# Mamba scan loop: the C rows by broadcast DMA from a DRAM scratch in place of a spread on TensorE and a copy on ScalarE

## Chip, cores and metric

The kernel runs on one core of a Trainium2 chip. The metric is device microseconds of one execution, the median of several. Engines: TensorE (PE in the rows; PEld is its weight load), VectorE (DVE), ScalarE (ACT), GpSimd (POOL), and the sync engine SP, which here only issues DMAs.

## What is computed

The reference is a network of four layers, each a mixer and an expert part. The change lies in the first mixer, a Mamba block on x of shape (2, 1024, 128) with 256 channels and 16 states:

```python
x_dbl = xs @ x_proj_w.T                       # 256 -> 64 + 16 + 16
dt, Bm, Cm = jnp.split(x_dbl, [DT_RANK, DT_RANK + D_STATE], axis=-1)
dt = jax.nn.softplus(dt @ dt_proj_w.T + dt_proj_b)
A = -jnp.exp(A_log)
def step(h, inp):
    dt_s, B_s, C_s, x_s = inp
    dA = jnp.exp(dt_s[..., None] * A)
    h = h * dA + (dt_s * x_s)[..., None] * B_s[:, None, :]
    y = jnp.einsum('bds,bs->bd', h, C_s)
    return (h, y)
...
y = jnp.transpose(ys, (1, 0, 2)) + D_param * xs
```

## The kernel before

Channels lie on the 128 partitions, the 2048 tokens (two sequences of 1024) along the row; four blocks of 512 tokens are called k = 0 to 3, a PSUM bank holds one block. Each engine has its own hand-written program; semaphores of the group m0 tie them together. `m0["dve"]`, `m0["act"]` and `m0["pe"]` are counters with named offsets.

Ahead of the scan, per block k: TensorE projects xs (L379) into two banks, 64 rows of dt and 32 rows of B and C. ACT copies dt to `dt_low` (L458). VectorE splits the 32 rows into three bf16 parts in `parts` (L548 to L552, the semaphore value `bc`), whose sum is the fp32 value. The banks are used in turn, so blocks 2 and 3 wait for block 0 and 1 to be read. Then ACT loads the table for exp and ln (L459). For each of eight (block, channel half) pairs TensorE projects dt (L389), ACT makes log(1 + exp(-|x|)) with three instructions (L467 to L469) and VectorE finishes delta with two (L561, L562). Four products `dtx` (L566) follow, delta times xs.

The scan loop has 64 units (b, m, n): sequence, channel half, state; each covers 128 channels and 1024 tokens. In one unit:

- TensorE spreads row n of B to all 128 partitions: two matmuls (one per half of the tokens) of a 0/1 selector with `parts` (L395), into the banks BMM; then likewise row n of C, into the banks CMM.
- ACT makes the decay exp(delta A) in two PSUM banks (L479), and copies the C banks to one of two buffers CB in `shared` (L484).
- VectorE makes the drive, dtx times B (L573), and the scan (L576), in one of four state buffers.
- GpSimd multiplies the states with C (L592).
- TensorE adds the product up in PSUM with an identity (L405, fp32), over the 16 states of a (b, m).

VectorE may reuse a state buffer when the sum of the unit four before is made; ACT copies a sum out every 16 units. After the loop come the skip term and the gate (L579, L580) and the output projection. SP loads later weights into `shared` after the gate.

## Time and profile before

| | us |
|---|---|
| median of 3 runs | 1453.62 |
| lowest, highest | 1451.54, 1453.8 |
| the profiled execution | 1451.61 |
| its span | 1449.9 |
| scan loop, first drive to last scan's end | 250.2 to 477.1 |

The span is the time from the first to the last instruction of the profiled execution. The times in rows are from its start; "idle before" is how long an engine stood still ahead of an instruction, and behind the arrow is what it waited for. TensorE's clock is given as a share of 2.4 GHz. fp32 matmuls appear as two instructions each.

### The profile page before, as it was taken

The page shows a single profiled execution, that of the slowest core. Times are in us where ns is not written, and L with a number is a line of the kernel's source. Part 1 is how long each engine was busy: PE and PEld are TensorE (multiplying, and loading weights), DVE is VectorE, ACT ScalarE, POOL GpSimd, SP SyncE. Part 2 cuts the span into 40 slices and gives each one's busy share as a digit, 9 for nine tenths or more (in the row PEclk, how much of TensorE's full clock was granted, in tenths as well). Part 3 has the DMA queues.
Part 4 walks back from the last instruction along what each step waited for, and adds up shares of the span by engine and source line. Part 5 has one row for each costly group of instructions (what it writes and reads, how often), then busy time and mean ns, then how long its engine had stood idle before and what let it go on. Part 6 is the DMA issues. An engine that isn't in the chain of part 4 may idle for free.

```text
span 1449.9 us, 14958 instructions
## 1 busy us (share of the span) xinstructions
PE 1249.0 (86%) x5185; PEld 623.9 (43%) x5185; DVE 1042.3 (72%) x1535; ACT 825.7 (57%) x1061; POOL 442.5 (31%) x231
## 2 busy tenths in 40 slices
PE   5889976888888659999995799999999999888887
PEld 1333321222222234544452566666656666522454
DVE  4555468999999846464346889999989999833354
ACT  4434455565565224342235778888888888644642
POOL 9000000666666830000000135454444545510000
PEclk8899997999999859999997899999999999999999
DMA  3000000000000300000000000000000000000000
GB/s 109 1 0 0 1 0 1 0 0 0 1 0 0 137 0 0 1 0 1 0 0 0 10 18 19 14 20 14 19 14 20 14 20 20 1 0 0 0 1 30
DMA packets 12043, 17.65 MB, mean 12 GB/s; under 512 B 3936, under 2 KB 9472, under 8 KB 11712
## 3 DMA queue, kind: packets, MB, share of 16 engines
q1 hardware_dynamic: 11968, 16.69, 3.7%
q8 instruction: 42, 0.69, 0.2%
q14 instruction: 33, 0.27, 0.1%
HBM read 14.85 MB, written 1.05 MB: 11 GB/s over the span
## 4 chain that ended last, share of the span: by engine, by line
PE 45%; DVE 34%; ACT 14%; issue 5%; POOL 1%; DMA 0%; DVEq 0%; POOLq 0%; SPq 0%; ACTq 0%
DVE work L576 10%; DVE work L1362 6%; DVE work L1381 5%; ACT ps L479 5%; PE ps L860 4%; PE ps L868 4%; PE ps L1016 4%; PE ps L876 4%; ACT work L1223 3%; DVE yd L1426 3%; ACT work L1218 2%; PE ps L640 2%; PE ps L1057 2%; DVE work L1429 2%; PE ps L654 2%
## 5 line engine op out<-in xcount | busy, mean ns | idle before, releaser
L592 POOL TENSOR_TENSOR work<-work,shared 128x1024 f32<-128x1024 f32 x64 | 151.7, 2370 | 237.9 <-DVE work L576 237.9
L576 DVE TENSOR_TENSOR_SCAN work<-ps,work 128x1024 f32<-128x1024 f32 x64 | 146.6, 2291 | 8.8
L1483 POOL TENSOR_TENSOR ssum<-ssum,rs 128x1024 f32<-128x1024 f32 x32 | 77.1, 2409 | 221.3 <-DVE work L1362 219.0
L1362 DVE SCALAR_TENSOR_TENSOR work<-work,w_t 128x1024 f32<-128x1024 f32 x96 | 123.4, 1285 | 24.2 <-ACT work L1223 21.9
L405 PE MATMUL ps<-work,ident 128*128 128x512 f32 x256 | 122.7, 602 | 5.0 <-POOL work L592 4.1
L479 ACT ACTIVATE ps<-work,A 128x1024 f32<-128x1024 f32 x64 | 71.6, 1118 | 97.1 <-DVE work L576 95.6
L395 PE MATMUL ps<-parts,sel 96*128 96x512 bf16 x256 | 79.4, 396 | 46.0 <-DVE work L573 24.4
L892 ACT ACTIVATE work<-ps 128x512 f32<-128x512 f32 x64 | 38.2, 597 | 108.7 <-PE ps L860 108.7
L1491 POOL TENSOR_TENSOR yd<-yd,work 128x896 f32<-128x896 f32 x32 | 67.0, 2094 | 71.6 <-DVE work L1429 71.6
L928 DVE TENSOR_TENSOR work<-work,ps 128x512 f32<-128x512 f32 x64 | 44.0, 688 | 55.3 <-PE ps L868 55.3
L1405 DVE SCALAR_TENSOR_TENSOR work<-work,ps 128x64 f32<-128x64 f32 x384 | 79.3, 276 | 6.1
L1381 DVE TENSOR_TENSOR work<-ps,work 128x512 f32<-128x512 f32 x128 | 79.3, 683 | 0.0
L573 DVE TENSOR_TENSOR work<-work,ps 128x1024 f32<-128x1024 f32 x64 | 76.6, 1197 | 0.1
L1494 POOL TENSOR_TENSOR work<-yd,work 128x1024 f32<-128x1024 f32 x32 | 75.5, 2359 | 2.5
L1414 DVE SCALAR_TENSOR_TENSOR work<-work 128x1024 f32<-128x1024 f32 x64 | 75.4, 1220 | 0.0
L1477 POOL MEMSET ssum<- 128x2048 f32 x1 | 1.8, 1805 | 238.7 <-DVE work L255 238.7
L1241 ACT ACTIVATE work<-ps 128x512 f32<-128x512 f32 x128 | 72.8, 596 | 2.0 <-PE ps L1033 1.7
L395 PEld LDWEIGHTS ps<-parts,sel 96*128 96x128 bf16 x256 | 15.7, 99 | 130.6 <-DVE work L573 74.2
L1022 PE MATMUL ps<-work,w_t 128*128 128x512 f32 x128 | 62.1, 609 | 9.5 <-ACT work L1218 9.5
L1080 PE MATMUL ps<-work,wo_t 128*128 128x512 f32 x128 | 64.7, 629 | 2.6 <-POOL work L1494 2.6
L405 PEld LDWEIGHTS ps<-work,ident 128*128 128x128 f32 x256 | 44.1, 191 | 52.9 <-issue 31.3
L1057 PE MATMUL ps<-work 128*128 128x128 f32 x448 | 63.7, 282 | 3.0 <-DVE work L1381 0.5
(337 smaller groups left out, 2719.8 us busy)
## 6 DMA issues: line engine op xcount, KB each, us to landing
w_t<-in_tile_w SPq DMA_DIRECT2D x32, 195.5 KB, 2.4
work<-in_w SPq DMA_DIRECT2D x1, 2048.0 KB, 9.8
shared<-in_f SPq DMA_DIRECT2D x3, 512.0 KB, 5.9
work<-in_x SPq DMA_DIRECT2D x4, 256.0 KB, 3.6
work<-in_w2e SPq DMA_DIRECT2D x1, 1024.0 KB, 11.8
spent<-work SPq DMA_DIRECT2D x64, 6.0 KB
sel<-parts SPq DMA_DIRECT2D x64, 6.0 KB
out_x<-work SPq DMA_DIRECT2D x4, 256.0 KB, 2.3
```

The source lines that it names most:

```text
L395: mm = pe.matmul(ps[:, bank + h, :], sel[:, first + n, :], parts[:, b * SEQ + h * BL:b * SEQ + (h + 1) * BL], start=True, stop=True)
L405: mm = pe.matmul(ps[:, YACC + h, :], ident[:, :], HS[u % 4][:, h * BL:(h + 1) * BL], start=(n == 0), stop=(n == DS - 1))
L479: act.activation(pair(DABANK), in_halves(DL[:, MI * b + m, :]), ACT.Exp, scale=A[:, m * DS + n:m * DS + n + 1]).then_inc(m0["decay"], 1)
L573: dve.tensor_tensor(h, DX[:, MI * b + m, :], flat_pair(BMM), ALU.mult).then_inc(m0["drive"], 1)
L576: dve.tensor_tensor_scan(h, flat_pair(DABANK), h, 0.0, ALU.mult, ALU.add).then_inc(m0["scan"], 1)
L592: pool.tensor_tensor(HS[u % 4], HS[u % 4], CB[u % 2], ALU.mult).then_inc(m0["state"], 1)
L1057: mm = pe.matmul(four(MID + k)[:, c % 4, :], BT[:, b * TB + c, :], HDD[:, c * P:(c + 1) * P], start=True, stop=True)
L1362: c = dve.scalar_tensor_tensor(HC[u], HP[:, tap:tap + SEQ], par(u, "taps", tap), HC[u], ALU.mult, ALU.add)
L1381: dve.tensor_tensor(heads(dst)[:, chunks], ps[:, FRONT + k, :].rearrange("p (c h q) -> p c h q", h=2, q=P2), bc3, ALU.mult).then_inc(done, 1)
L1405: part = dve.scalar_tensor_tensor(ST[:, c, cols], ST[:, c - 1, cols], CDEC[:, b * TB + c, 2 * t + h:2 * t + h + 1], four(MID + k)[:, c % 4 ...
L1483: pool.tensor_tensor(ssum[:, b, :], ssum[:, b, :], rs[:, :, :].rearrange("p k t -> p (k t)"), ALU.add).then_inc(m2["ss"], 1)
L1494: pool.tensor_tensor(Y[u], YD[:, :], SG[u], ALU.mult).then_inc(m2["y"], 1)
```

## The change

The spread of C on TensorE and the copy of it on ACT go. In their place:

- ACT copies the 32 rows of B and C of each block from PSUM to `bc_whole` (the first 32 partitions of slot 1), behind the copy of dt of the same block and after VectorE's split of it. TensorE, which reuses the banks, waits for that copy too (`c_out`).
- SP stores the four blocks to a DRAM scratch `bc_rows` of 32 x 2048 fp32, then, once delta is complete, loads for each unit row 16 + n, 1024 tokens, to all 128 partitions: 512 KB, in one of three buffers (two in `shared`, one in `yd`). From the fourth unit on it waits for GpSimd's product three units back.
- GpSimd waits for the load (`c_in0` to `c_in2`) in place of ACT's copy. VectorE waits once, before the loop, for the four stores (`c_rows`), since slot 1 also holds two of the state buffers.

B still comes from TensorE.

```diff
+        bc_rows = nc.dram_tensor("bc_rows", [2 * DS, T], F32, kind="Internal").ap()
...
-        CB = [shared[:, 0:SEQ], shared[:, SEQ:2 * SEQ]]
-        BMM, CMM, DABANK, YACC = 0, 2, 4, 6
+        CB = [shared[:, 0:SEQ], shared[:, SEQ:2 * SEQ], YD[:, :]]
+        BMM, DABANK, YACC = 0, 4, 6
+        c_in = [m0["c_in0"], m0["c_in1"], m0["c_in2"]]
+        bc_whole = slot(1)[0:2 * DS, :]
...
                     pe.wait_ge(m0["act"], m0["xd_out"] + k - 1)
+                    pe.wait_ge(m0["c_out"], k - 1)
...
-                    spread(u + 1, 0, BMM, m0["b_mm"])
-                    pe.wait_ge(m0["c_ready"], u + 1)
-                    spread(u + 1, DS, CMM, m0["c_mm"])
+                    spread(u + 1)
...
                 act.activation(blk(dt_low, k), ps[0:DR, 2 * (k % 2), :], ACT.Copy).then_inc(m0["act"], 1)
+                act.wait_ge(m0["pe"], m0["xd"] + 2 * k + 2)
+                act.wait_ge(m0["dve"], m0["bc"] + k + 1)
+                act.activation(blk(bc_whole, k), ps[0:2 * DS, 2 * (k % 2) + 1, :], ACT.Copy).then_inc(m0["c_out"], 1)
...
-                act.wait_ge(m0["c_mm"], u + 1)
-                if u >= 2:
-                    act.wait_ge(m0["state"], u - 1)
-                act.activation(in_halves(CB[u % 2]), pair(CMM), ACT.Copy).then_inc(m0["c_ready"], 1)
...
             dve.wait_ge(m0["dve"], m0["dtx"] + BATCH * MI)
+            dve.wait_ge(m0["c_rows"], 16 * NB)
...
-                pool.wait_ge(m0["c_ready"], u + 1)
-                pool.tensor_tensor(HS[u % 4], HS[u % 4], CB[u % 2], ALU.mult).then_inc(m0["state"], 1)
+                pool.wait_ge(c_in[u % 3], 16 * (u // 3 + 1))
+                pool.tensor_tensor(HS[u % 4], HS[u % 4], CB[u % 3], ALU.mult).then_inc(m0["state"], 1)
...
+            for k in range(NB):
+                sp.wait_ge(m0["c_out"], k + 1)
+                sp.dma_start(bc_rows[:, k * BL:(k + 1) * BL], blk(bc_whole, k)).then_inc(m0["c_rows"], 16)
+            sp.wait_ge(m0["c_rows"], 16 * NB)
+            sp.wait_ge(norm["out"], NB * 3)
+            sp.wait_ge(m0["dve"], m0["delta"] + MI * NB)
+            for u, (b, _, n) in enumerate(UNITS):
+                if u >= 3:
+                    sp.wait_ge(m0["state"], u - 2)
+                sp.dma_start(CB[u % 3], bc_rows[DS + n:DS + n + 1, b * SEQ:(b + 1) * SEQ].to_broadcast([P, SEQ])).then_inc(c_in[u % 3], 16)
```

How the instructions stand, first on ACT between the convolution and the first triple of the delta stage. Before:

```order
L455 ACTIVATE work<-work 128x1024 [waits m0_dve] x4
L458 ACTIVATE work<-ps 64x512 [waits m0_pe] x4
L459 ACT_TABLE_LOAD
L467 ACTIVATE work<-ps,vec 128x512 [waits m0_pe]
L468 ACTIVATE work<-work 128x512 [waits act_own]
```

After:

```order
L455 ACTIVATE work<-work 128x1024 [waits m0_dve] x4
L458 ACTIVATE work<-ps 64x512 [waits m0_pe]
L461 ACTIVATE work<-ps 32x512 [waits m0_dve,m0_pe]
L458 ACTIVATE work<-ps 64x512 [waits m0_pe]
L461 ACTIVATE work<-ps 32x512 [waits m0_dve,m0_pe]
L458 ACTIVATE work<-ps 64x512 [waits m0_pe]
L461 ACTIVATE work<-ps 32x512 [waits m0_dve,m0_pe]
L458 ACTIVATE work<-ps 64x512 [waits m0_pe]
L461 ACTIVATE work<-ps 32x512 [waits m0_dve,m0_pe]
L462 ACT_TABLE_LOAD
L470 ACTIVATE work<-ps,vec 128x512 [waits m0_pe]
```

A copy of the B and C rows (L461), which waits for VectorE, now stands behind each copy of dt, and all four stand ahead of the table load.

On TensorE, one unit of the loop (spreads, and the add-up of the unit two back). Before:

```order
L395 MATMUL ps<-parts,sel 128x512 [waits m0_drive]
L395 MATMUL ps<-parts,sel 128x512
L395 MATMUL ps<-parts,sel 128x512 [waits m0_c_ready]
L395 MATMUL ps<-parts,sel 128x512
L405 MATMUL ps<-work,ident 128x512 [waits m0_state]
L405 MATMUL ps<-work,ident 128x512
```

After, with the head of the next unit:

```order
L399 MATMUL ps<-parts,sel 128x512 [waits m0_drive]
L399 MATMUL ps<-parts,sel 128x512
L408 MATMUL ps<-work,ident 128x512 [waits m0_state]
L408 MATMUL ps<-work,ident 128x512
L399 MATMUL ps<-parts,sel 128x512 [waits m0_drive]
```

The second pair of spreads, with its wait for ACT's copy, is gone.

On SP, from the last of the early loads to the later weights. Before:

```order
L1718 DMA w_sw<-in_sw 64x128
L1719 DMA dtr<-in_dt_row 128x96
L1722 DMA shared<-in_w_bc 128x256 [waits m0_dve]
L1722 DMA shared<-in_ew 128x512 x2
L1722 DMA shared<-in_qkv 128x384
```

After:

```order
L1719 DMA dtr<-in_dt_row 128x96
L1721 DMA bc_rows<-work 32x512 [waits m0_c_out] x4
L1729 DMA shared<-bc_rows 128x1024 [waits m0_dve,norm_out,m0_c_rows]
L1729 DMA shared<-bc_rows 128x1024
L1729 DMA yd<-bc_rows 128x1024
L1729 DMA shared<-bc_rows 128x1024 [waits m0_state] x2
L1729 DMA yd<-bc_rows 128x1024 [waits m0_state]
```

Four stores and 64 loads stand between the early and the later loads.

## Rows read from the trace of the kernel before

**Rows 1.** The page, busy us (share of the span) and instructions of each engine

```profile
PE 1249.0 (86%) x5185; PEld 623.9 (43%) x5185; DVE 1042.3 (72%) x1535; ACT 825.7 (57%) x1061; POOL 442.5 (31%) x231
```

**Rows 2.** The page's costliest groups: count | busy us, mean ns | idle before, releaser

```profile
L592 POOL TENSOR_TENSOR work<-work,shared 128x1024 f32<-128x1024 f32 x64 | 151.7, 2370 | 237.9 <-DVE work L576 237.9
L576 DVE TENSOR_TENSOR_SCAN work<-ps,work 128x1024 f32<-128x1024 f32 x64 | 146.6, 2291 | 8.8
...
L573 DVE TENSOR_TENSOR work<-work,ps 128x1024 f32<-128x1024 f32 x64 | 76.6, 1197 | 0.1
```

**Rows 3.** Timeline of one unit: start us, us, engine, line, operation [idle before]

```profile
441.56 1.20 DVE L573 TENSOR_TENSOR work<-work,ps 128x1024 f32<-128x1024 f32 x1
...
442.73 1.00 ACT L484 ACTIVATE shared<-ps 128x1024 f32<-128x1024 f32 x1
...
442.81 0.60 PE L395 MATMUL ps<-parts,sel 96*128 96x512 bf16 x2 [0.24 <-DVE work L573]
442.90 2.29 DVE L576 TENSOR_TENSOR_SCAN work<-ps,work 128x1024 f32<-128x1024 f32 x1
...
444.23 1.88 PE L405 MATMUL ps<-work,ident 128*128 128x512 f32 x4
...
445.10 1.20 DVE L573 TENSOR_TENSOR work<-work,ps 128x1024 f32<-128x1024 f32 x1
```

**Rows 4.** Line L573: duration ns min/median/max, first and last start us

```profile
L573 DVE TENSOR_TENSOR work<-work,ps x64: 1194/1197/1222, 250.2 to 473.5; 128x1024 f32<-128x1024 f32 x64
```

**Rows 5.** Timeline of ACT ahead of the delta stage

```profile
218.21 1.05 ACT L458 ACTIVATE work<-ps 64x512 f32<-64x512 f32 x2
222.08 0.59 ACT L458 ACTIVATE work<-ps 64x512 f32<-64x512 f32 x1 [2.82 <-PE ps L379]
225.78 0.59 ACT L458 ACTIVATE work<-ps 64x512 f32<-64x512 f32 x1 [3.10 <-PE ps L379]
226.38 1.28 ACT L459 ACT_TABLE_LOAD   x1
228.66 0.69 ACT L467 ACTIVATE work<-ps,vec 128x512 f32<-128x512 f32 x1 [1.00 <-PE ps L389]
```

**Rows 6.** VectorE in that stretch, and one wait (us in total, times, longest)

```profile
219.31 0.68 DVE L552 TENSOR_TENSOR parts<-work,part_tmp 32x512 bf16<-32x512 f32 x1
...
222.22 0.68 DVE L552 TENSOR_TENSOR parts<-work,part_tmp 32x512 bf16<-32x512 f32 x1
223.92 0.68 DVE L548 CAST parts<-ps 32x512 bf16<-32x512 f32 x1 [1.02 <-PE ps L379]
...
229.80 0.68 DVE L552 TENSOR_TENSOR parts<-work,part_tmp 32x512 bf16<-32x512 f32 x1
...
245.51 4.63 DVE L566 TENSOR_TENSOR work<-work 128x1024 f32<-128x1024 f32 x4
...
DVE work L561 <- ACT work L469: 3.2, 8, 0.4
```

**Rows 7.** TensorE in that stretch: the projections of blocks 2 and 3

```profile
220.14 7.43 PE L379 MATMUL ps<-work,w_x_proj 128*64 128x512 f32 x16 [2.05 <-DVE parts L552]
```

**Rows 8.** DMAs: count, KB each, median us to landing; and the sum of 490 to 506 us

```profile
shared<-in_f SPq DMA_DIRECT2D x3, 512.0 KB, 5.9
...
dtr<-in_dt_row SPq DMA_DIRECT2D x1, 48.0 KB, 3.0
...
DMA packets 1416, 4.89 MB, mean 306 GB/s; under 512 B 156, under 2 KB 648, under 8 KB 1160
```

**Rows 9.** Stretches: PE, PEld, DVE, ACT, POOL busy (count), PE clock, DMA share, GB/s

```profile
250.00:260.00 10.00, 6.99 (x12) 2.19 (x13) 9.65 (x7) 4.12 (x4) 4.72 (x2) 0.50 0.00 1
...
820.00:830.00 10.00, 7.36 (x66) 5.36 (x65) 9.17 (x9) 7.82 (x8) 0.89 (x1) 1.00 0.02 4
```

**Rows 10.** The chain of work that ended last, at the loop's start

```profile
254.89 2.02 PE ps L395 x4
256.91 3.41 PE ps L405 x4
```

More of the change, by code:

```diff
@@ L207, in build @@
                     dve="weff:1 gated:8 x1:4 peak:1 scaled:4 conv:4 bc:4 delta:8 dtx:4 ygate:4 s_out:4",
-                    each="gamma b_mm c_mm c_ready ysum decay drive scan state")
+                    each="gamma b_mm c_out c_rows c_in0 c_in1 c_in2 ysum decay drive scan state")
         f0 = stages("f0", pe="logit:4 probs_T:1 picked_T:1 vT:1 mix:4", act="lg:4 exps:2 v_out:1 g:4",
@@ L390, in l0_pe, with spread @@
                               start=True, stop=True).then_inc(m0["pe"], 1)
-            def spread(u, first, bank, mm_sem):
+            def spread(u):
                 b, _, n = UNITS[u]
                 for h in range(2):
-                    mm = pe.matmul(ps[:, bank + h, :], sel[:, first + n, :],
-                                   parts[:, b * SEQ + h * BL:b * SEQ + (h + 1) * BL], start=True, stop=True)
-                mm.then_inc(mm_sem, 1)
+                    mm = pe.matmul(ps[:, BMM + h, :], sel[:, n, :], parts[:, b * SEQ + h * BL:b * SEQ + (h + 1) * BL], start=True, stop=True)
+                mm.then_inc(m0["b_mm"], 1)
             def add_up(u):
@@ L410, in l0_pe @@
             pe.wait_ge(const["ready"], 3)
-            spread(0, 0, BMM, m0["b_mm"])
-            spread(0, DS, CMM, m0["c_mm"])
+            spread(0)
             for u in range(len(UNITS)):
@@ L1451, in stairs @@
             pool.wait_ge(m0["b_mm"], len(UNITS))
-            pool.wait_ge(m0["c_mm"], len(UNITS))
+            pool.wait_ge(m0["state"], len(UNITS))
             own(pool.memset(causal[:, :], 1.0))
```

## Prediction

> **What bounds the kernel now.** I began with the busy shares of the page: TensorE is busy for 86% of the span, but that is a mean over many stages, and the change touches one stage, the scan loop of 64 units, and the stage ahead of it [rows 1]. The three groups of the loop say what its limit is [rows 2]: one unit costs VectorE 1.197 us (drive, L573) and 2.291 us (scan, L576), 3.488 us together, and GpSimd only 2.370 us (L592), before which it sat idle for 237.9 us waiting for the scan. The timeline of one unit [rows 3] gives the period: L573 starts at 441.56 and again at 445.10, 3.54 us. L576 starts 0.14 us after L573 ends and the next L573 starts as the scan ends. Over the loop it is the same: first and last L573 at 250.2 and 473.5 us [rows 4], 223.3 us for 63 periods, 3.544 us each. VectorE leaves 0.056 us of a period unused, so nothing taken off another engine can shorten this loop. Ahead of the loop I read the three engines side by side from 216 us on [rows 5 to 7], and the list of waits for that stretch [rows 6]: VectorE waited for ACT before each of the eight L561. So from 228.66 us, where ACT starts its first L467, to the loop, ACT's chain of eight triples sets the time.
>
> **What leaves the loop.** Per unit two spreads on TensorE (0.60 us for the pair, the L395 row at 442.81) and one copy on ACT (1.00 us, L484) go away [rows 3]. Over 64 units that is 38 us of TensorE and 64 us of ACT, and all of it lies beside VectorE's 3.49 us. ACT's exponential (L479) starts on the scan's end, and the drive of 1.197 us covers it. TensorE's add-up takes 1.88 us at full clock [rows 3] and is needed only four units later. Gain: 0.
>
> **What enters the loop.** A load of 512 KB per unit into one of three buffers, used by GpSimd. First its lead. Load u is issued when GpSimd ends unit u-3 and is needed when GpSimd starts unit u: 3 x 3.54 - 2.37 = 8.3 us [rows 2, 3]. The nearest loads in size and shape are the three in_f: 512 KB in 4 KB pieces, median 5.9 us to landing with others around them [rows 8]. That is inside 8.3 us. The first load is issued when the last delta is there and needed after dtx (4.63 us, L566), a drive and a scan: 4.63 + 1.2 + 2.3 = 8.1 us, also enough [rows 2, 6, 8]. If it were late, the four state buffers let VectorE run on: it would notice a lateness only when it outgrew about 6 us (unit u waits for the sum of unit u-4, ready 3 x 3.54 - 1.2 - 3.1 = 6.3 us early, where 3.1 is the 1.2 us left of GpSimd's product after the drive and the 1.88 us of add-up).
> Then its rate. To keep up, 524,288 bytes must move per 3.54 us, 148 GB/s. Fast end: in 16 us around the largest loads the queue moved 4.89 MB at a mean of 306 GB/s [rows 8], so 1.7 us a load. Slow end: that a load holds the queue for the whole 5.9 us that an in_f took. No row shows a large load whose 128 partitions all read the same 4 KB; the only broadcast load is 48 KB (3.0 us, in_dt_row) [rows 8], too small to tell a rate from a latency. I take the fast end, since in_f has the same piece size, bytes and issuing queue, and keep the slow end as a rival. Price taken: 0.
> The Trainium skill has a measurement that speaks against this: "DMA: Bandwidth & Descriptors", section "Latency and other measured facts", tells that copies whose 128 partition rows lie a large power of two apart in DRAM fell to 103 GB/s, and supposes that streams in lock step fall on the same memory channel. A distance of zero might do the same; by its figure my estimate is 5.1 us a load and a sum higher by some 99 us. No row here shows it either way.
>
> **What enters ahead of the loop.** This is where I find a cost. ACT gets four copies of 32x512, one behind each L458, and each waits for the split on VectorE of the same block (L548 to L552). A copy is priced by L458, 64x512, 0.59 us [rows 5]; for a 32-row copy of the same width that is the upper side, and 0.4 us lower cannot be excluded.
> Step 1: the split of block 0 ends at 219.31 + 0.68 = 219.99 [rows 6]. TensorE started block 2 on that, at 220.14 [rows 7]. Now it waits for the copy behind it as well, about 220.05 to 220.64, so block 2 starts at 220.78, 0.64 us later. Block 3 is not held again: the split of block 1 ends at 222.22 + 0.68 = 222.90 [rows 6] and the copy behind it at 223.5, when TensorE is still in block 2 (7.43 us for both blocks, so 3.7 us from 220.78) [rows 7]. The splits of blocks 2 and 3 wait for TensorE (the one of block 2 had sat idle 1.02 us for it), so they move along, and the last ends at 229.80 + 0.68 + 0.64 = 231.12 [rows 6].
> Step 2: before, ACT was through with its last L458 at 226.37, loaded its table (1.28 us) in the shadow and waited 1.00 us for TensorE, then began at 228.66 [rows 5]. Now the last copy can't start before 231.17, ends at 231.76, and the table load stands behind it in program order: 233.04. The first triple starts at about 233.1, 4.4 us later than 228.66. Nothing covers that: VectorE has no other work than the eight L561/L562 pairs, and before each it waits for ACT [rows 6]; its eight triples fill the 16.9 us from 228.66 to the first dtx at 245.51 without slack, so nothing catches up. So dtx and the loop start 4.4 us later. Bounds: 3.8 (a copy at 0.3 us, twice in the chain) and 4.9 (some 0.1 us more at each of five hand-overs).
> Step 3: four stores of 64 KB to the scratch. The last is issued at about 231.8; VectorE asks for them at the first drive, some 22 us later. Price 0; SP has nothing else queued there, and its later weight loads wait for the gate (L580) after the loop as before. A C load's issue holds SP well under a period.
>
> **TensorE's clock at the loop's start.** At 250 to 260 us the granted clock is 0.50 of full, the 1.2 GHz level; the longer stretch at 2.4 GHz follows [rows 9]. On the lower level the add-up took 3.41 us and the four spreads 2.02 us [rows 10], so a unit now needs 3.41 + 1.01 = 4.42 us instead of 5.43, still more than 3.54. TensorE will be full and the clock should rise as it did, perhaps a few us later for the lighter first units; each further unit on the lower level costs at most 0.88 us. I take 0, and 0 to 1 us for the range. Later a unit needs 2.48 us of 3.54, 70%. The nearest row, 820 to 830 us, is busy for 7.36 of 10 us and keeps 1.00 [rows 9].
>
> **Sum.** 0 (loop) + 4.4 (ACT's chain) + 0 (stores) + 0 (clock) = +4.4 us, made against the profiled execution, 1451.61 us with a span of 1449.9. That one lies 2.0 us under the median of the runs, 1453.62. The same addition gives 1456.0 for it and **1458.0 us** for the median, 0.3% slower.
>
> **The rivals.**
> A. The broadcast loads are the bound. They decide from 3.54 us of queue time per load, under 148 GB/s; then the three buffers and the four states run out and VectorE idles at every drive. At 5.9 us a load [rows 8] it is 64 x (5.9 - 3.54) = +151 us, 1609 us with the 4.4. For it: all 16 engines read one 4 KB row, which no row here shows. Against: 306 GB/s for other loads leaves a factor of two. Chance 0.11. The Trainium skill's figure above would put this case at about 1557 us, as an estimate.
> B. Not slower: ACT's late start is absorbed and the time stays at 1453.6, because the copies run earlier than I read (each right behind its L458) or VectorE catches up in the eight pairs. It decides if the last copy and table load end by 228.7. For it: before, ACT had idled 2.82 and 3.10 us there. Against: the copies wait for the splits, which end at 231.1. Chance 0.09.
> C. TensorE's clock falls back in the loop, since it idles twice in each unit. At worst the lower level holds throughout: 64 x 0.88 = +56 us, 1514 us. Against: at the lower level it would be full, and full stretches run at 1.00 here. Chance 0.03.
>
> **How the numbers follow.** My forecast has 0.77; its own range is 1456.5 to 1460.5 (3.8 to 4.9 us, up to 1 us for the clock, about 1 us for the spread of the medians). Rival B pulls the low end to 1452.5, and a few slow-clock units, or loads a few hundredths of a us over the period, the high end to 1466; A and the bad half of C stay out, about 0.13. A measurement of this kernel can tell about 0.2%, 2.9 us, from no change, so slower begins at 1456.5. Of my forecast 0.72 lies above that; with A and C, slower has 0.85. Same is 0.13, faster 0.02, for which I know no mechanism.
>
> **What would show it.** Right: the first L467 (now L470) near 233.1 us with ACT idle ahead of the copies, waiting for VectorE; the period of the drives still 3.54 us; no VectorE idle in the loop; GpSimd waiting for the scan and not for a DMA; C loads landing under 8.3 us, at 148 GB/s over the loop. Wrong: a period over 3.54 us with waits on the loads (A), a first L467 before 230 us (B), a clock under 1.00 in the loop (C), or VectorE and GpSimd instructions longer while the loads write their memory.

## The result, and the profile after

The changed kernel takes 1460.34 us (median of 8 runs, 1456.51 to 1461.11), the kernel before 1453.71 us (8 runs, 1451.54 to 1457.28). The ratio is 1.004, with a 95% interval of 1.0026 to 1.0053: slower by 3.8 to 7.7 us. The profiled execution took 1459.21 us with a span of 1457.5 us, 7.6 us more than before on both counts.

First the busy times, which answer to [rows 1]. The page of the changed kernel:

```profile
PE 1225.8 (84%) x5057; PEld 615.1 (42%) x5057; DVE 1039.5 (71%) x1535; ACT 768.0 (53%) x1001; POOL 442.2 (30%) x231
```

TensorE lost 23 us of work and ACT 58 us, and the kernel is slower. (From 250 to 478 us the spreads fell from 77.5 to 39.0 us, the 38 us that the prediction had taken off; TensorE's total fell by less, and its add-ups alone took 7 us more, 129.6 in place of 122.7.) The loop tells why VectorE has nothing of this. These are its costliest groups on the page (they answer to [rows 2]), and then line L573 by itself (to [rows 4]):

```profile
L576 DVE TENSOR_TENSOR_SCAN work<-ps,work 128x1024 f32<-128x1024 f32 x64 | 146.6, 2291 | 9.0
...
L573 DVE TENSOR_TENSOR work<-work,ps 128x1024 f32<-128x1024 f32 x64 | 76.5, 1196 | 0.0
```

```profile
L573 DVE TENSOR_TENSOR work<-work,ps x64: 1194/1195/1221, 254.3 to 477.5; 128x1024 f32<-128x1024 f32 x64
```

The drives run from 254.3 to 477.5 us, 223.2 us for 63 periods. Before it was 223.3 us. VectorE's two instructions have kept their length, and nothing stands between them. The loop as a whole has only moved to a later place.

That move comes from ahead of the loop. The timeline of ACT in the changed kernel (start, length, idle before and what it waited for), to be held against [rows 5]:

```profile
216.72 1.06 ACT L455 ACTIVATE work<-work 128x1024 f32<-128x1024 f32 x1 [3.63 <-DVE work L538]
217.68 0.57 ACT L458 ACTIVATE work<-ps 64x512 f32<-64x512 f32 x1
...
219.56 0.59 ACT L461 ACTIVATE work<-ps 32x512 f32<-32x512 f32 x1 [1.30 <-DVE parts L551]
...
230.84 0.59 ACT L461 ACTIVATE work<-ps 32x512 f32<-32x512 f32 x1 [2.63 <-DVE parts L551]
231.44 1.28 ACT L462 ACT_TABLE_LOAD   x1
232.74 0.69 ACT L470 ACTIVATE work<-ps,vec 128x512 f32<-128x512 f32 x1
```

TensorE and VectorE in the same stretch, to be held against [rows 6, 7]:

```profile
220.40 7.43 PE L383 MATMUL ps<-work,w_x_proj 128*64 128x512 f32 x16 [2.80 <-ACT work L461]
...
230.06 0.68 DVE L551 TENSOR_TENSOR parts<-work,part_tmp 32x512 bf16<-32x512 f32 x1
...
254.26 1.22 DVE L573 TENSOR_TENSOR work<-work,ps 128x1024 f32<-128x1024 f32 x1
```

Each new copy waits for the split (L551) of its block, and the table load stands behind the last copy. From the first copy of dt to the first triple it is 232.74 - 217.68 = 15.06 us; before it was 228.66 - 218.21 = 10.45 us. From the first triple to the first drive it is 254.26 - 232.74 = 21.52 us, as before (250.18 - 228.66). So this stage costs +4.61 us, and no later work of the stage caught any of it up. In absolute time the loop starts 4.1 us later, since this execution reached the stage 0.5 us earlier.

The loads, which no row of before could show. The page's DMA groups, and the sum for 250 to 490 us:

```profile
shared<-bc_rows SPq DMA_DIRECT2D x43, 512.0 KB, 3.5
...
yd<-bc_rows SPq DMA_DIRECT2D x21, 512.0 KB, 3.6
```

```profile
DMA packets 9225, 33.66 MB, mean 140 GB/s; under 512 B 1024, under 2 KB 1024, under 8 KB 9216
```

A load lands in 3.5 to 3.6 us at the median (the longest in 5.8 us), inside its lead of 8.3 us. The mean of 140 GB/s is taken over a window somewhat longer than the loop; over a period it is 148. GpSimd's idle time is still put down to the scan alone:

```profile
L592 POOL TENSOR_TENSOR work<-work,shared 128x1024 f32<-128x1024 f32 x43 | 102.1, 2374 | 217.6 <-DVE work L576 217.6
```

TensorE's clock, in the windows that answer to [rows 9] (PE, PEld, DVE, ACT, POOL busy and counts, PE clock, DMA share, GB/s):

```profile
250.00:260.00 10.00, 2.06 (x4) 0.26 (x4) 9.79 (x8) 1.83 (x2) 2.11 (x1) 0.50 0.47 158
260.00:270.00 10.00, 8.51 (x19) 3.00 (x18) 9.57 (x7) 3.35 (x3) 6.43 (x4) 0.85 0.47 156
300.00:310.00 10.00, 7.13 (x18) 1.98 (x17) 9.57 (x7) 3.35 (x3) 7.06 (x3) 1.00 0.46 157
```

It starts the loop on the lower level, 1.2 GHz, and then stays at 2.4 GHz although TensorE is now busy for only 71% of the time.

**The rest of the 7.6 us.** The stage costs 4.6 of the 7.6 us between the two profiled executions. I followed the same instruction in both traces from the loop on. The lag of the changed kernel is 4.0 us at the end of the loop and 4.9 us from 547 to 662 us. Then it jumps. VectorE in the kernel before:

```profile
662.59 0.29 DVE L833 TENSOR_SCALAR wvs<-w_wvT,ps 128x128 f32<-128x128 f32 x1 [2.71 <-PE ps L793]
...
675.82 0.29 DVE L836 TENSOR_TENSOR wcomb<-w_wq,ps 128x128 f32<-128x128 f32 x1 [1.25 <-PE ps L797]
```

The same two instructions in the changed kernel:

```profile
667.45 0.29 DVE L833 TENSOR_SCALAR wvs<-w_wvT,ps 128x128 f32<-128x128 f32 x1 [2.71 <-PE ps L793]
...
682.38 0.29 DVE L836 TENSOR_TENSOR wcomb<-w_wq,ps 128x128 f32<-128x128 f32 x1 [1.25 <-PE ps L797]
```

The lag grows from 4.86 to 6.56 us between them, on code that the change doesn't touch. The windows show what differs. Before, and then after, for the 5 us around that work:

```profile
670.00:675.00 5.00, 5.00 (x13) 2.23 (x13) 2.29 (x4) 1.19 (x2) 0.00 (x0) 1.00 0.01 3
```

```profile
674.90:679.90 5.00, 5.00 (x9) 2.12 (x9) 1.29 (x3) 1.19 (x2) 0.00 (x0) 0.66 0.00 0
```

TensorE is full in both, with a granted clock of 1.00 before and 0.66 after, and so gets through 9 matmuls where it had got through 13. From there the lag falls to 5.5 us, since the kernel before has such a stretch of its own (clock 0.66 from 745 to 750 us, where the changed kernel has 1.00), and it ends at 7.7 us from 1362 us on, behind another one (clock 0.66 from 1355 to 1360 us). One pair of executions can't say whether the change causes this or whether each execution has it somewhere else; the table behind E7 bears on that.

### The profile page after: what moved, and what is told of

The parts are those of the page before. It is cut to its first block, busy times and chain, and to the rows that moved or that the text cites. A ratio compares the mean times of both kernels' runs of the same rounds, so it can differ in the third digit from the quotient of the medians.

```text
span 1457.5 us, 14655 instructions
## 1 busy us (share of the span) xinstructions
PE 1225.8 (84%) x5057; PEld 615.1 (42%) x5057; DVE 1039.5 (71%) x1535; ACT 768.0 (53%) x1001; POOL 442.2 (30%) x231
## 4 chain that ended last, share of the span: by engine, by line
PE 44%; DVE 35%; ACT 15%; issue 5%; POOL 1%; DMA 0%; DVEq 0%; POOLq 0%; SPq 0%; ACTq 0%
DVE work L576 10%; DVE work L1362 6%; DVE work L1381 5%; ACT ps L482 5%; PE ps L860 4%; PE ps L868 4%; PE ps L1016 4%; PE ps L876 4%; ACT work L1223 3%; DVE yd L1426 3%; ACT work L1218 2%; PE ps L640 2%; PE ps L1057 2%; DVE work L1429 2%; PE ps L654 2%
## 5 line engine op out<-in xcount | busy, mean ns | idle before, releaser
L408 PE MATMUL ps<-work,ident 128*128 128x512 f32 x256 | 129.6, 630 | 47.3 <-POOL work L592 47.3
L592 POOL TENSOR_TENSOR work<-work,shared 128x1024 f32<-128x1024 f32 x43 | 102.1, 2374 | 217.6 <-DVE work L576 217.6
L892 ACT ACTIVATE work<-ps 128x512 f32<-128x512 f32 x64 | 38.2, 597 | 111.5 <-PE ps L860 111.5
L573 DVE TENSOR_TENSOR work<-work,ps 128x1024 f32<-128x1024 f32 x64 | 76.5, 1196 | 0.0
L860 PE MATMUL ps<-work 128*128 128x512 f32 x128 | 66.4, 643 | 0.0
L1072 PEld LDWEIGHTS ps<-work 128*64 128x64 f32 x1024 | 55.3, 137 | 24.9 <-issue 24.9
```

Source lines behind the costliest of these rows:

```text
L408: mm = pe.matmul(ps[:, YACC + h, :], ident[:, :], HS[u % 4][:, h * BL:(h + 1) * BL], start=(n == 0), stop=(n == DS - 1))
L573: dve.tensor_tensor(h, DX[:, MI * b + m, :], flat_pair(BMM), ALU.mult).then_inc(m0["drive"], 1)
L592: pool.tensor_tensor(HS[u % 4], HS[u % 4], CB[u % 3], ALU.mult).then_inc(m0["state"], 1)
L860: pe.matmul(ps[:, 1 + m, :], W["w13"][:, c:c + P], blk(XN, k), start=True, stop=True).then_inc(f1["gate"], 1)
```

## The experiments

Two theories. Mine: the whole steady cost is the chain of copy, wait and table load ahead of the loop, and the loads cost nothing. The rival: the loads take a part, by being late or by contention, and the later start is one share among others.

**E1, the copies alone.** The kernel before, with the four copies and the waits on them, and nothing else:

```diff
                     pe.wait_ge(m0["act"], m0["xd_out"] + k - 1)
+                    pe.wait_ge(m0["c_out"], k - 1)
...
+                act.wait_ge(m0["pe"], m0["xd"] + 2 * k + 2)
+                act.wait_ge(m0["dve"], m0["bc"] + k + 1)
+                act.activation(blk(bc_whole, k), ps[0:2 * DS, 2 * (k % 2) + 1, :], ACT.Copy).then_inc(m0["c_out"], 1)
...
+            dve.wait_ge(m0["c_out"], NB)
```

> The kernel before, with only the four copies of the B and C rows (32x512) added on ACT, each behind the split of its block, and TensorE waiting for them; the loop is that of before and nothing is stored or loaded. Theory (ACT's chain ahead of the loop is the whole cost): from the first copy of dt (L458) to the first drive (L573) 36.6 us as in the changed kernel, against 31.97 before; the time about 4.6 us over before. Rival 1 (part of the 6.6 us between the medians comes from the DMAs, in the loop or behind it): this stretch 36.6 us too, but the time clearly nearer to before than the changed kernel's, by 2 us or more. Rival 2 (the copies are hidden, the stores cost): stretch 32 us, time as before.

Measured: 1458.82 us (median of 10 runs, 1454.76 to 1461.47), ratio 1.003 (1.0009 to 1.0051), profiled span 1456.4 us. The copies alone make the kernel slower, without one load. The median lies 5.0 us over the kernel before, and that of the changed kernel 6.6 us; rival 1 had asked for a gap of 2 us or more, and the intervals are too wide to exclude one. The stage was even longer than expected, 38.2 us from the first copy of dt (217.62) to the first drive, where 36.6 follow from the chain. Timeline of this kernel:

```profile
220.34 9.08 PE L381 MATMUL ps<-work,w_x_proj 128*64 128x512 f32 x16 [3.04 <-ACT work L463]
...
255.85 1.22 DVE L579 TENSOR_TENSOR work<-work,ps 128x1024 f32<-128x1024 f32 x1
```

The projections of blocks 2 and 3 took 9.08 us here and 7.43 us before and after. The window says why:

```profile
220.00:225.00 5.00, 4.66 (x7) 1.00 (x8) 2.18 (x5) 1.63 (x4) 0.00 (x0) 0.66 0.00 0
```

The granted clock was 0.66 in these 5 us, behind a wait of 3.04 us, where the changed kernel had 2.80 us of wait and kept its speed. The copies lengthen TensorE's pause ahead of block 2 (before, it was 2.05 us [rows 7]), and in this execution a lower clock followed. That is a second price beside the chain's, 1.65 us, and an unsteady one: the changed kernel's trace doesn't have it, while that of E7, with the same stage, has it again.

**E2, the loads alone.** The changed kernel without copies, stores and their waits; the loads read rows of an input tensor:

```diff
-                    pe.wait_ge(m0["c_out"], k - 1)
...
-                act.wait_ge(m0["pe"], m0["xd"] + 2 * k + 2)
-                act.wait_ge(m0["dve"], m0["bc"] + k + 1)
-                act.activation(blk(bc_whole, k), ps[0:2 * DS, 2 * (k % 2) + 1, :], ACT.Copy).then_inc(m0["c_out"], 1)
...
-                sp.dma_start(CB[u % 3], bc_rows[DS + n:DS + n + 1, b * SEQ:(b + 1) * SEQ].to_broadcast([P, SEQ])).then_inc(c_in[u % 3], 16)
+                sp.dma_start(CB[u % 3], a["w13"][DS + n:DS + n + 1, b * SEQ:(b + 1) * SEQ].to_broadcast([P, SEQ])).then_inc(c_in[u % 3], 16)
```

> The changed kernel without the copies and the stores: the 64 broadcast loads take rows of an input weight matrix instead of the scratch (so the C values are wrong, size and shape of each load are kept). Theory: stretch from first copy of dt to first drive 32.0 us, period of the drives 3.544 us, time as before within 0.2%. Rival 1 (the DMAs cost something): a period over 3.55 us, or the loop as before but the stages behind it later by 2 us or more than in the kernel before.

Measured: 1457.95 us (median; 1451.14 to 1459.55), 1453.86 for the kernel before, ratio 1.0015 (0.9991 to 1.0038); the profiled execution 1451.44 us with a span of 1449.7 us, that of before to 0.2 us. Lines of its trace, ACT's timeline and line L567, the drive:

```profile
217.79 1.05 ACT L456 ACTIVATE work<-ps 64x512 f32<-64x512 f32 x2
```

```profile
L567 DVE TENSOR_TENSOR work<-work,ps x64: 1195/1195/1220, 249.8 to 473.0; 128x1024 f32<-128x1024 f32 x64
```

From the first copy of dt to the first drive it is 31.97 us (217.79 to 249.76), to the hundredth what it was before (218.21 to 250.18), and the loop takes 223.2 us. So in stage and loop the loads cost nothing. For the whole kernel this is not shown. The median lies 4.1 us over before, and the interval, -1.3 to +5.5 us, contains nothing at all as well as a cost as large as that of the copies. Six of the ten runs took 1457.90 us or more, and 5 of the 31 runs of the kernel before in the same session. The profiled execution lies at the fast end of this kernel's runs, and its total equals that of before only because stretches behind the loop cancel (table behind E7). So rival 1, in its part on the stages behind the loop, stays open.

**E3, the table load first.** The changed kernel, with the table load ahead of the four copies:

```diff
+            act.preload_act_table_set("natural_log_exp_and_others")
             for k in range(NB):
...
-            act.preload_act_table_set("natural_log_exp_and_others")
```

> The changed kernel with the load of ACT's table for exp and ln moved ahead of the copies, where ACT idles. Theory (the table load stands in the chain behind the last copy): the first triple starts 1.3 us earlier after the first copy of dt than in the changed kernel (13.8 us in place of 15.06), the stretch to the first drive 35.3 us, the time 1.3 us under the changed kernel's. Rival 2 (something else delays the triples, such as TensorE's projection): 15.06 us as before, no change.

ACT and then VectorE in the timeline of this kernel:

```profile
216.82 1.06 ACT L455 ACTIVATE work<-work 128x1024 f32<-128x1024 f32 x1 [3.63 <-DVE work L538]
217.89 1.28 ACT L456 ACT_TABLE_LOAD   x1
...
230.94 0.59 ACT L462 ACTIVATE work<-ps 32x512 f32<-32x512 f32 x1 [2.63 <-DVE parts L551]
231.43 0.66 ACT L470 ACTIVATE work<-ps,vec 128x512 f32<-128x512 f32 x1
...
252.92 1.22 DVE L573 TENSOR_TENSOR work<-work,ps 128x1024 f32<-128x1024 f32 x1
```

The same activation (L455) in the kernel before:

```profile
217.25 1.06 ACT L455 ACTIVATE work<-work 128x1024 f32<-128x1024 f32 x1 [3.63 <-DVE work L539]
```

The first triple follows directly on the last copy. From the last activation ahead of the stage (216.82 us) to the first drive it is 36.10 us; in the changed kernel 37.54 (216.72 to 254.26), before 32.93 (217.25 to 250.18). So the table load was worth 1.4 us of the 4.6. The whole doesn't show it: 1459.44 us (1454.51 to 1461.92), ratio 1.0023 (1.0005 to 1.0041), span 1457.7 us, and the trace gives the 1.4 us back behind the loop, where TensorE runs on a lower clock than in the changed kernel (0.67 against 1.00 from 755 to 760 us).

**E4, each copy one place later.** The copy of block k stands behind the dt copy of block k+1, and that of block 3 behind the first triple:

```diff
+                if k >= 1:
+                    bc_out(k - 1)
...
+                    if n == 0:
+                        bc_out(NB - 1)
```

> The changed kernel with the copies one block later in ACT's order (copy of block k behind the copy of dt of block k+1, the last one behind the first triple of the delta stage), so that ACT does not stand at the split of the last block. Loads and stores are unchanged. Theory: of the 4.6 us about 1.2 stay (0.7 since TensorE's block 2 still waits for the first copy, 0.5 for the copy between the triples): stretch from first copy of dt to first drive 33.2 us, time 3.4 us under the changed kernel's and 1.2 us over before. Rival 1 (the DMAs carry part of the loss): the stretch shortens as said but the time stays 3 us or more over before.

The timeline of ACT, and the first drive:

```profile
216.78 1.06 ACT L455 ACTIVATE work<-work 128x1024 f32<-128x1024 f32 x1 [3.63 <-DVE work L544]
...
227.20 0.59 ACT L459 ACTIVATE work<-ps 32x512 f32<-32x512 f32 x1 [0.52 <-DVE parts L557]
227.81 1.28 ACT L466 ACT_TABLE_LOAD   x1
229.10 0.69 ACT L474 ACTIVATE work<-ps,vec 128x512 f32<-128x512 f32 x1
...
231.02 0.57 ACT L459 ACTIVATE work<-ps 32x512 f32<-32x512 f32 x1
...
251.09 1.22 DVE L579 TENSOR_TENSOR work<-work,ps 128x1024 f32<-128x1024 f32 x1
```

From 216.78 us, the last activation, to the first drive it is 34.31 us: 1.4 us over before, 3.2 us under the changed kernel. The same four copies of the same data, with the same waits, lose two thirds of their price by their place in ACT's order. The median is 1456.94 us (1454.96 to 1460.42), ratio 1.0015 (0.9998 to 1.0032). It lies 3.1 us over before where 1.2 us was expected, and rival 1 had named 3 us or more; with an interval of -0.3 to +4.7 us the time decides between neither. The stage does, for itself.

**E5 and E6, fewer buffers.** One or two buffers for C in place of three; the load then waits for the product one or two units back:

```diff
-                pool.tensor_tensor(HS[u % 4], HS[u % 4], CB[u % 3], ALU.mult).then_inc(m0["state"], 1)
+                pool.tensor_tensor(HS[u % 4], HS[u % 4], CB[u % 1], ALU.mult).then_inc(m0["state"], 1)
...
-                if u >= 3:
-                    sp.wait_ge(m0["state"], u - 2)
+                if u >= 1:
+                    sp.wait_ge(m0["state"], u - 0)
```

> The changed kernel with one buffer for the C rows in place of three. Theory (a load needs issue-to-landing time, here 3.5 us, inside the lead that the ring leaves): the lead is 3.54 - 2.37 = 1.2 us, so the loads become the bound and a unit takes product + landing + hand-over = 2.37 + 3.5 + 0.1 = 6.0 us; the loop 64 x 6.0 = 383 us, the time 156 us over the changed kernel's, near 1615 us. Rival (loads are bound by bandwidth, so the number of buffers matters little): period under 4.5 us.

> The changed kernel with two buffers for the C rows. Theory: the lead is 2 x 3.54 - 2.37 = 4.7 us, more than the 3.5 us of a load, so the period of the drives stays 3.544 us and GpSimd waits for the scan as before; the time as the changed kernel's within its scatter. Rival (the slowest loads, up to 5.8 us, set the pace): a period over 3.55 us with GpSimd waiting for loads.

E5 took 1617.46 us in its one execution (expected: near 1615). GpSimd in its trace:

```profile
301.22 2.34 POOL L592 TENSOR_TENSOR work<-work,shared 128x1024 f32<-128x1024 f32 x1 [3.77 <-DMA shared<-bc_rows]
307.33 2.35 POOL L592 TENSOR_TENSOR work<-work,shared 128x1024 f32<-128x1024 f32 x1 [3.77 <-DMA shared<-bc_rows]
```

This period is 307.33 - 301.22 = 6.11 us: a product of 2.35 and the load's whole way of 3.77 us. Over the loop (first product at 259.9, last at 640.5 us) it is 6.04 us, and 6.0 was expected. This is what a loop looks like that the loads bound: GpSimd's idle time is put down to a DMA. E6 took 1459.47 us, also in one execution, and its drives run from 254.4 to 477.7 us, 223.3 us. With two buffers the lead is 2 x 3.54 - 2.37 = 4.7 us, against 3.5 us to landing, and that is enough. The third buffer buys nothing in these traces.

**E7, twice the loads.** The changed kernel, with a second load of the same size in each unit, to memory that nobody reads:

```diff
+                if u >= 2:
+                    sp.wait_ge(m0[f"twin{u % 2}"], 16 * (u // 2))
+                sp.dma_start(S[:, (u % 2) * SEQ:(u % 2 + 1) * SEQ], bc_rows[n:n + 1, b * SEQ:(b + 1) * SEQ].to_broadcast([P, SEQ])).then_inc(m0[f"twin{u % 2}"], 16)
```

> The changed kernel with a second broadcast load of 512 KB per unit (the B row of the unit, to an idle buffer that nobody reads), 296 GB/s in place of 148. Theory (a broadcast from one 4 KB row runs as fast as other loads, some 300 GB/s or more): the period stays at 3.54 us or goes a little over, to 3.6 us; landing rises to 4 to 6 us. Rival (rows that all partitions read at once are limited to about 103 to 200 GB/s): the period goes to 5 us and more, the time over 1550 us.

The queue from 262 to 470 us (packets, MB, share of the 16 engines), and line L573:

```profile
q1 hardware_dynamic: 16873, 61.46, 86.6%
```

```profile
L573 DVE TENSOR_TENSOR work<-work,ps x64: 1194/1195/1222, 255.4 to 478.6; 128x1024 f32<-128x1024 f32 x64
```

61.46 MB in 208 us are 296 GB/s, and the loop still takes 223.2 us. The changed kernel uses half of this. VectorE's drive has a median of 1195 ns with the doubled traffic as without, so the writes into the memory it works on don't slow it either. The C loads landed in 3.6 to 3.7 us at the median, the second ones in 4.9. The one execution took 1457.08 us.

The same trace has the stage of the changed kernel once more, and here the projections are as slow as in E1:

```profile
219.91 9.08 PE L383 MATMUL ps<-work,w_x_proj 128*64 128x512 f32 x16 [2.99 <-ACT work L461]
```

The granted clock from 220 to 225 us is 0.66 again. From the first copy of dt (217.19) to the first drive (255.40) it is 38.2 us, as in E1 and 1.6 us more than in the changed kernel's trace. So the change can have either price.

**Behind the loop, in all these traces.** VectorE's program behind the loop is the same in every kernel, so each of its instructions can be compared with itself. How many us later than in the kernel before it starts, at five places given by their time in the kernel before:

| | end of the loop | 655 us | 690 us | 820 us | the end |
|---|---|---|---|---|---|
| changed kernel | 4.0 | 4.9 | 6.6 | 6.0 | 7.7 |
| E1, copies alone | 5.6 | 7.2 | 7.2 | 5.8 | 6.6 |
| E2, loads alone | -0.5 | -1.4 | 0.3 | -0.9 | -0.1 |
| E3, table first | 2.7 | 2.3 | 4.0 | 6.3 | 7.9 |
| E4, late copies | 0.8 | 1.8 | 3.5 | 2.9 | 4.6 |
| E6, two buffers | 4.2 | 5.1 | 6.8 | 6.3 | 7.9 |
| E7, twice the loads | 5.1 | 5.2 | 5.2 | 5.2 | 5.5 |

Between 655 and 690 us the lag grows by 1.7 us or not at all. E2 has the step without the copies, and E7 lacks it with copies, stores and loads. So no part of the change brings it each time, and the execution of the kernel before that all are measured against is one without it. Whether the change, or the loads alone, make such steps more frequent can't be read from one trace a kernel.

**What the freed engine time is good for.** The loop is bound by VectorE's drive and scan, 3.49 of 3.54 us, and the change frees ACT, TensorE and two PSUM banks. V1 puts them to use: every fourth drive goes to GpSimd, with B also by broadcast load; the decay gets a second pair of banks, so that the exponential no longer waits for the scan of the unit before; the copies stand as in E4.

```diff
-        BMM, DABANK, YACC = 0, 4, 6
+        BMM, DABANKS, YACC = 0, (4, 2), 6
+        POOLED_U = [u for u in range(len(UNITS)) if u % 4 == 3]
...
-                if u >= 1:
-                    act.wait_ge(m0["scan"], u)
+                if u >= 2:
+                    act.wait_ge(m0["scan"], u - 1)
...
+                pool.tensor_tensor(HS[w % 4], DX[:, MI * b + m, :], BB[i % 2], ALU.mult).then_inc(m0["pdrive"], 1)
```

> A version that uses what the change makes possible: the copies one block later as in the run with late copies; in every fourth unit GpSimd, not VectorE, makes the drive, from a B row that is also loaded by broadcast (SBUF to SBUF, 2.37 us a drive), one unit group ahead; the two PSUM banks that the C spread left free hold a second decay buffer, so ACT's exponential does not wait for the last scan. Theory (VectorE bounds the loop, the scratch and the freed banks are slack): four units cost VectorE 4 x 2.29 + 3 x 1.2 + about 0.25 = 13.0 us in place of 14.18, GpSimd 5 x 2.37 = 11.9, so the loop takes 208 us in place of 227; ahead of it +1.4 us; the time 17 us under before, near 1437 us. Rival (VectorE and GpSimd get in each other's way when GpSimd reads two SBUF operands more often, or the loads at 202 GB/s are late): a period of four units over 13.5 us.

Measured: 1449.87 us (median of 10, 1447.78 to 1454.01), ratio 0.9967 (0.9949 to 0.9986). A gain, but a small one, 5 us in place of the expected 17. The list of waits from 262 to 470 us (us in total, times, longest) and one place of the timeline:

```profile
DVE work L586 <- PE ps L404: 18.8, 15, 2.7
```

```profile
305.56 1.22 DVE L586 TENSOR_TENSOR work<-work,ps 128x1024 f32<-128x1024 f32 x1 [2.07 <-PE ps L404]
```

A new wait had taken the place of the old one. Behind each drive of GpSimd, VectorE waits for TensorE's spread of B, which stands in TensorE's order behind an add-up that waits for GpSimd. V2 orders the spread right behind VectorE's drive before:

```diff
-                if u + 1 in DRIVES:
+                nxt = [x for x in DRIVES if x > u][:1]
+                if u in DRIVES and nxt:
...
-                    spread(u + 1)
+                    spread(nxt[0])
```

> The version in which GpSimd makes every fourth drive, with one more edit: TensorE spreads the B row of the next unit that VectorE drives as soon as the bank is free, ahead of the add-ups. In the version before it VectorE waited 18.8 us in 15 groups of units for that spread, which stood behind an add-up that waited for a late product. Theory (that order was what ate the gain): the wait goes, four units take 13.0 us, the loop 208 us in place of 220.5, the time 12 us less, near 1438 us. Rival (VectorE then waits for GpSimd's drive or for the sums, which come late too): four units over 13.5 us.

> The same kernel as v2_spread_early, timed again on the chip of v4_one_decay_buffer and with more rounds, since v2 has few runs behind its interval. Theory: 1432.7 us as before, within 1 us, with four units of the loop in 12.49 us. Rival: the first look was a lucky one and the scatter that the other kernels show (several us from where TensorE's lower clock falls behind the loop) puts it at 1436 to 1440 us.

Measured: 1432.73 us (4 runs, 1431.95 to 1435.26), ratio 0.9842 (0.9799 to 0.9884), and the same kernel again 1433.83 us (5 runs, 1432.81 to 1435.56), ratio 0.9858 (0.9834 to 0.9883). It takes about 20 us less than the kernel before and 27 us less than the changed one, and more was gained than expected, since four units take 12.49 us and not 13.0. Its waits from 262 to 440 us, and a group of four units in VectorE's timeline:

```profile
DVE work L587 <- PE ps L404: 1.9, 4, 0.5
```

```profile
302.14 1.20 DVE L587 TENSOR_TENSOR work<-work,ps 128x1024 f32<-128x1024 f32 x1
...
310.24 4.47 DVE L592 TENSOR_TENSOR_SCAN work<-ps,work 128x1024 f32<-128x1024 f32 x2
...
314.63 1.20 DVE L587 TENSOR_TENSOR work<-work,ps 128x1024 f32<-128x1024 f32 x1
```

Four units take 314.63 - 302.14 = 12.49 us where they took 4 x 3.543 = 14.17.

V3 gives GpSimd every third drive, by one edit of that list (`u % 3 == 2`):

> The same with every third drive on GpSimd. Theory (both engines then carry the same load): three units cost VectorE 3 x 2.29 + 2 x 1.2 + 0.2 = 9.5 us and GpSimd 4 x 2.36 = 9.4 us, so the loop takes 64 / 3 x 9.5 = 202 us, 6 us less than with every fourth; near 1432 us. The loads run at 222 GB/s. Rival (with no slack on GpSimd its lateness adds up and VectorE waits): no gain over every fourth, or a loss.

Measured: 1445.94 us (6 runs, 1442.45 to 1447.66), ratio 0.9929 (0.9904 to 0.9955), a miss: 13 us over V2, where 6 us less had been expected. Waits, and the window of 300 to 350 us, here and then in V2:

```profile
DVE work L587 <- PE ps L404: 12.4, 13, 1.1
```

```profile
300.00:350.00 50.00, 37.54 (x80) 14.32 (x79) 43.83 (x25) 16.49 (x15) 44.92 (x20) 0.88 0.58 202
```

```profile
300.00:350.00 50.00, 38.51 (x88) 13.13 (x86) 49.14 (x29) 18.81 (x17) 45.72 (x20) 0.97 0.59 206
```

VectorE, the bound in V2 with 49.14 of 50 us, is down to 43.83, and waits for TensorE. TensorE's granted clock is 0.88 against 0.97, with about the same busy time for fewer matmuls. Whether GpSimd's late products lengthen TensorE's pauses and the clock follows, or the clock comes first, was not settled.

V4 is V2 with a single pair of decay banks, so it does without the two banks that the change freed:

```diff
-        BMM, DABANKS, YACC = 0, (4, 2), 6
+        BMM, DABANKS, YACC = 0, (4, 4), 6
...
-                if u >= 2:
-                    act.wait_ge(m0["scan"], u - 1)
+                if u >= 1:
+                    act.wait_ge(m0["scan"], u)
```

> This is v2 (every fourth drive by GpSimd, the next spread ordered right behind the last drive of VectorE) with one decay buffer in place of two, so it no longer uses the two PSUM banks that the change has freed. The exponential of the next unit then waits for the scan again. It tells whether v2's gain needs those banks. Theory: it needs them. In v2 four units take 12.49 us: three drives of 1.20, two scans of 2.29 with a hand-over of 0.14 or less, and two scans back to back of 4.47. With one decay buffer the exponential (1.12 us and some 0.3 us of hand-overs) stands open between those two scans, once in four units, where no drive covers it: 12.49 + 1.4 = 13.9 us, against 14.16 us for four units of the changed kernel. Loop about 225 us, execution about 1455 us (v2: 1432.7; before 1453.6). Rival: the gain comes from taking drives off VectorE alone, the banks don't matter: 1433 us, four units in 12.5 us. The rival would also mean that the kernel before could have had this gain without the change.

Measured: 1460.59 us (10 runs, 1452.2 to 1461.37), ratio 1.0025 (1.0002 to 1.0047). VectorE's timeline:

```profile
302.56 1.20 DVE L587 TENSOR_TENSOR work<-work,ps 128x1024 f32<-128x1024 f32 x1
...
307.45 2.29 DVE L592 TENSOR_TENSOR_SCAN work<-ps,work 128x1024 f32<-128x1024 f32 x1 [1.25 <-ACT ps L494]
...
316.74 1.20 DVE L587 TENSOR_TENSOR work<-work,ps 128x1024 f32<-128x1024 f32 x1
```

Four units take 14.18 us, as if all the drives were still VectorE's: where a drive has left VectorE, the exponential that it used to hide stands open. So the gain of V2 needs the second pair of banks. It follows that the change, which by itself costs some microseconds, is what makes room for a version that gains. (Whether another way of using the banks of the kernel before would gain as much was not tried.)

## Why the prediction came out as it did

- **Nothing leaves the path in the loop**: right. 23 us of TensorE and 58 us of ACT are gone, and the 63 periods take 223.2 us in place of 223.3. (The prediction had 38 and 64 us. The spreads did fall by 38, while TensorE's add-ups took 7 us more; on ACT the new copies take 2 us of the 64 back, and the rest of the difference was not followed up.)
- **The loads are hidden**: right for the stage and the loop, and shown from three sides. They land in 3.5 us of an 8.3 us lead, two buffers are enough (E6), and the queue carries twice the bytes (E7). Rival A needs under 148 GB/s; E7 moved 296. The near row, 306 GB/s for the loads of 490 to 506 us, was the right guide. The slow end, that a load holds the queue for the 5.9 us that an in_f took to land, did not come about: with two loads in each period of 3.54 us they landed in 3.6 to 4.9 us.
- **The figure that spoke against it**: the Trainium skill's 103 GB/s ("DMA: Bandwidth & Descriptors", section "Latency and other measured facts"), for partition rows that lie a large power of two apart in DRAM, does not carry over to a distance of zero: 128 partitions that read one 4 KB row had 296 GB/s in E7. Its own case was not run here.
- **The chain ahead of the loop**: right in mechanism, 0.2 us too small. Measured from the first copy of dt, block 2 starts 0.79 us later and not 0.64 (220.40 - 217.68 against 220.14 - 218.21), because TensorE starts 0.25 us after the end of ACT's copy (219.56 + 0.59 = 220.15) where it had started 0.15 us after the end of VectorE's split. From the start of the last split to the first triple it is 2.68 us (230.06 to 232.74), and was -1.14 (229.80 to 228.66): 3.82 us, as in step 2. Together 4.61, predicted 4.4. Rival B needed the table load to end by 228.7 us; it ended at 232.7. E3 and E4 show the parts: the table load behind the copies 1.4 us; with each copy one place later, and the table load no longer behind the last of them, 3.2 us are gone. What the prediction had not priced is that the longer pause ahead of block 2 can be followed by a lower clock there, 1.65 us more in E1 and E7 and nothing in the changed kernel's trace.
- **Nothing catches up**: right. The 21.52 us from the first triple to the first drive are the same.
- **The clock in the loop**: right, a price of 0. It rose some microseconds into the loop and stayed at 1.00. The fall that rival C named does exist nearby: in E5, with its period of 6.04 us, the granted clock from 262 to 600 us is 0.67.
- **The stores**: a price of 0, right. The first drive comes 21.5 us after the first triple in both kernels.
- **What the sum left out**: the measured difference of the medians is 6.6 us and that of the profiled executions 7.6 us, against 4.6 us that the stage shows. The interval of the ratio (3.8 to 7.7 us) contains 4.6. In the profiled pair the surplus arises in code that the change doesn't touch, at stretches where TensorE was granted less clock. E1 and E7 had such a stretch in the stage itself, right behind a pause that the copies lengthen, which speaks for a share of the copies. The stretches far behind the loop come and go: E7, with the whole change, carries its lag of 5.1 us from the loop to the end and adds 0.3, and E2, without the copies, has one of the steps. The kernel before itself took 1450.76 to 1460.35 us over all the sessions. The steps may be a matter of the execution alone or be made more frequent by the change (7 of its 8 runs took 1459 us or more) or by the loads (E2's median). That stays open.
- **How far the number was luck**: the sum said 1458.0 us for the median and 1456.0 for the profiled execution; they came out at 1460.34 and 1459.21. The mechanism gives the first 4.6 of the 6.6 us. That the median still lies within the range, near its upper end, is in part luck: the range had been widened for a slow clock at the loop's start, which cost nothing, and for the spread of the medians, and what filled it was something else.

## What to carry to other kernels

Work taken off engines that only stand beside the bound gained nothing here, although it was 81 us; what counts is what the edit puts into the in-order programs of the engines on the way, and an instruction that waits, set ahead of a table load or a critical chain, holds back all that stands behind it (the same four copies cost 4.6 us in one place and 1.4 us in another). Ask of freed resources what they allow rather than what they save: two free PSUM banks let a quarter of VectorE's drives go to GpSimd, and that was 20 us. For a load into a ring of buffers compare the lead, buffers times period less the consumer's time, with the time to landing, and the bytes per period with the queue's rate; here two buffers met both, and one did not.

## What was not expected of the hardware

- Two scans in a row took 4.47 us in V2, 2.24 us each; alone a scan shows 2.29 us and starts 0.14 us after the drive that it waits for. A drive taken away saves more than its 1.20 us: 14.17 - 12.49 = 1.68 us.
- The ACT table load delayed its follower by its own length only: 231.44 + 1.28 = 232.72, and the next activation starts at 232.74. It had idled nothing ahead of it and nothing behind.
- TensorE's clock differed between nearly equal executions of one piece of work: a wait of 2.80 us ahead of the projections left them at 7.43 us (after), one of 3.04 us was followed by a clock of 0.66 and 9.08 us (E1), and so was one of 2.99 us (E7). E3 and E4, with waits of 2.85 and 2.84 us, kept 7.43 us. That the length of the wait decides is not shown by this; the granted clock ahead of the wait differed too (210 to 215 us: 0.87 in E1 and 0.90 in E7, 0.81 in the changed kernel).
- Runs of one kernel differ by several microseconds (1450.76 to 1460.35 us for the kernel before), and between traces the lag moves in steps of 1 to 2 us where TensorE's granted clock differs. E2's profiled execution equals that of before to 0.2 us, while its median lies 4 us above (whether by its loads or by chance stays open). A gain of 1 or 2 us in one stage (E3) is seen in a trace and not in the time of the whole.
